# First attention of a four-layer gated cross-attention network: averaging normalised tokens with a folded Wv·Wo, and summing the weights in the exponential

## The reference

```python
xn = layer_norm(ctx, gamma_x, beta_x)                   # 64 context tokens of a sequence
ln = layer_norm(layernorm(x), gamma_l, beta_l)          # 64 latent tokens
q = (ln @ Wq).reshape(b, 64, 8, 64)                     # 8 heads of 64
k_x, v_x = split(xn @ Wkv); k_l, v_l = split(ln @ Wkv)
k_x = rope_rotate(k_x)                                  # k*cos + rotate_half(k)*sin, context keys only
k = concat([k_x, k_l]); v = concat([v_x, v_l])          # 128 keys and values of a sequence
out = softmax(q @ k.T / 8) @ v                          # per head
x = x + tanh(g_xattn[0]) * (out.reshape(b, 64, 512) @ Wo)
```

## Time and profile before

| what | value |
|---|---|
| median of 3 runs | 2398.12 us |
| profiled execution, its own time | 2399.08 us |
| its span | 2397.3 us |
| mean granted TensorE clock | 0.94 |
| busy over the span | PE 87%, DVE 79%, ACT 51%, POOL 14% |
| the first attention | 36 to 695 us, 64 tiles |
| in 52 to 690 us of it | PE busy 635.7 of 638 us, DVE 570.4, ACT 321.5, clock 1.00 |

### The profile page before, as it was taken

How to read it: one execution, slowest core, us unless ns; L and a number is a source line. 1 busy time by engine, 2 the same in 40 slices (tenths; PEclk the granted TensorE clock), 3 DMA queues, 4 the chain that set the end, 5 groups by cost and what they waited for, 6 DMA issues and landing times. The chain is left out here.

```text
span 2397.3 us, 51278 instructions
## 1 busy us (share of the span) xinstructions
PE 2076.7 (87%) x16365; PEld 1539.6 (64%) x16365; DVE 1888.4 (79%) x5125; ACT 1226.7 (51%) x2434; POOL 340.5 (14%) x680
## 2 busy tenths in 40 slices
PE   3999999999977888999998979699999987499507
PEld 3888888888853435777775757477777765244207
DVE  3899999999969898888885779566666668787785
ACT  1455555555533335677675646354544445307737
POOL 0111111111114443111111114100000022200000
PEclk9999999999988789999998989799999999699859
DMA  6111111111100000111110001112112111002442
GB/s 178 46 46 46 45 45 45 45 45 45 46 18 1 0 0 19 24 24 24 23 23 5 0 17 55 71 72 106 71 74 103 71 37 36 1 0 100 182 139 70
DMA packets 118317, 119.72 MB, mean 50 GB/s; under 512 B 45001, under 2 KB 101218, under 8 KB 116194
## 3 DMA queue, kind: packets, MB, share of 16 engines
q1 hardware_dynamic: 112248, 116.10, 16.0%
q10 hardware_dynamic: 5994, 2.70, 0.4%
HBM read 76.56 MB, written 25.43 MB: 43 GB/s over the span
## 5 line engine op out<-in xcount | busy, mean ns | idle before, releaser
L1658 DVE TENSOR_TENSOR arena<-arena 128x512 f32<-128x512 f32 (+1 forms) x256 | 171.1, 686 | 65.3 <-ACT arena L1696 59.7
L1696 ACT ACTIVATE arena<-banks,b1c 128x512 f32<-128x512 f32 x192 | 131.7, 687 | 168.4 <-PE banks L1571 168.2
L656 ACT ACTIVATE arena<-arena 128x512 f32<-128x512 f32 x128 | 80.8, 631 | 193.0 <-DVE arena L604 193.0
L888 PE MATMUL banks<-we,arena 128*128 128x512 f32 x256 | 141.5, 708 | 22.6 <-ACT arena L804 20.9
L1581 PEld LDWEIGHTS banks<-w2a,arena 128*128 128x128 f32 x1024 | 124.1, 192 | 28.7 <-issue 28.7
L217 DVE TENSOR_SCALAR xhat<-x_tiles,mean_var,rstd 128x128 f32 (+1 forms) x320 | 107.9, 374 | 33.6 <-POOL rstd L762 28.3
L1146 ACT ACTIVATE arena<-arena 128x512 f32<-128x512 f32 x128 | 80.7, 631 | 100.0 <-DVE arena L1098 100.0
L502 PE MATMUL banks<-arena 128*128 128x128 f32 x1024 | 131.3, 281 | 0.1
L1024 PE MATMUL banks<-arena 128*128 128x512 f32 x256 | 125.9, 615 | 3.9 <-ACT arena L1152 0.2
L1092 DVE TENSOR_REDUCE arena<-banks 128x8 f32<-128x512 f32 x128 | 87.7, 685 | 51.5 <-PE banks L1024 51.4
L518 PE MATMUL banks<-arena,wk 128*128 128x128 f32 x1024 | 126.6, 277 | 1.1 <-DVE arena L626 1.1
(11 more groups left out here) (271 smaller groups left out, 5402.1 us busy)
## 6 DMA issues: line engine op xcount, KB each, us to landing
arena<-coef_scratch SPq DMA_DIRECT2D x16, 2048.0 KB, 7.1
arena<-arena SPq DMA_DIRECT2D x128, 128.0 KB, 2.3
gated_scratch<-arena SPq DMA_DIRECT2D x16, 768.0 KB, 3.3
arena<-gated_scratch SPq DMA_DIRECT2D x16, 768.0 KB, 4.3
arena<-z1T_scratch SPq DMA_DIRECT2D x128, 64.0 KB, 2.2
arena<-ctxT_scratch SPq DMA_DIRECT2D x32, 256.0 KB, 2.8
arena<-in_ctx SPq DMA_DIRECT2D x64, 64.0 KB, 1.8
z1T_scratch<-arena SPq DMA_DIRECT2D x64, 64.0 KB, 1.5
```

The source lines that it names most:

```text
L888: mm = pe.matmul(ps[:, 6 + t.par if h else 2 + j, :], xTg[g.par][:, j * P:(j + 1) * P], k.we0[:, 4 * h:4 * h + 4, :].rearrange("p e m -> p ...
L1658: dve.tensor_tensor(hT[g.par][rows, c, :], hT[g.par][rows, c, :], wide_coef[g.par][rows, e, :], ALU.mult).then_inc(s["scaled"].sem, 1)
L1696: act.activation(hT[g.par][:, c, :], ps[:, HID + c % NHID, :], ACT.Gelu, bias=k.b1c[:, c:c + 1])\
```

## The change

It touches the first attention, its weights and their preparation.

- **Values and projection.** The values are no longer computed. For each head the kernel averages the 128 normalised tokens z (64 context, 64 latent) with the softmax weights, Y_h = z^T P_h^T, and multiplies by a folded matrix Wvo_h = Wv_h Wo_h (128x128). `prepare` makes the eight Wvo_h with 8 products and two copies.
- **Sums.** The exponential is now one ACTIVATE for each pair of heads, 128 columns each, four for each sequence: it reads the scores from PSUM, takes the negative scaled maximum as a bias column and writes the row sum by `accum_out`. VectorE no longer subtracts the maximum; it scales it (128x4), takes the reciprocal of the sums (128x4) and multiplies the weights by it before the transpose.
- **Queries.** QBD is zeroed once; ScalarE copies the two 64-row halves of the queries into it, VectorE's masked multiply goes.
- **Rotation.** The columns of Wq and Wk stay in their order, so the swap exchanges 32-row blocks: four transfers of 32 rows instead of two of 64; the signs of the sine table follow.
- **Context.** The transposed context comes in as an input (`ctxT`); its transpose, copy and store in the stage go.
- **Order.** The transposes of the weights, their use and the projection move one step later, x is updated another step later (lag 2 on VectorE), and the order within each body is new. VectorE's order in step s is: x of tile s-2, affine outputs of s+1, statistics of s+2, maxima and their scaling for both sequences of s, normalised x and context of s+2, `normalise(s, 0)`, cosine part of s+1, `normalise(s, 1)`, sine part and sum of s+1. ScalarE's order is that of the last hunk below.

```diff
@@ prepare
+        act.wait_ge(folded, 3)
+        for n in range(2):
+            act.activation(k.wvo0[:, n::2, :], ps[:, n, :].rearrange("p (h d) -> p h d", d=D), ACT.Copy)\
+                .then_inc(turned_sb, 1)
...
-        for dst, src in ((k.wq0, wq_raw), (k.wk0, wk_raw)):
-            to = dst[:, :].rearrange("p (c s h i) -> p s c h i", s=2, h=2, i=HD0 // 2)
-            of = src.rearrange("p (c h s i) -> p s c h i", s=2, h=2, i=HD0 // 2)
-            for half in range(2):
-                dve.tensor_copy(to[:, half], of[:, half]).then_inc(built, 1)
...
+        for h in range(H0):
+            rows = slice(h % 2 * HD0, h % 2 * HD0 + HD0)
+            mm = pe.matmul(ps[:, h % 2, h // 2 * D:(h // 2 + 1) * D], wvT[rows, h // 2, :], wo_raw[rows, h // 2, :],
+                           start=True, stop=True)
+        mm.then_inc(folded, 1)
@@ attention0, sync
-                sp.wait_ge(*s["ctxT_sb"](t))
-                sp.dma_start(k.ctxT_dram[t.idx], cto[t.par]).then_inc(k.ctxT_stored.at(t), 16)
                 sp.wait_ge(*s["kc"](t))
                 if t.has(1):
                     sp.wait_ge(*s["ksin"](t.back(1)))
-                for to, of in ((slice(0, 64), slice(64, P)), (slice(64, P), slice(0, 64))):
-                    sp.dma_start(kr[to, :], kc[of, :]).then_inc(swapped.at(t), 16)
+                for n in range(4):
+                    to, of = n * 32, (n ^ 1) * 32
+                    sp.dma_start(kr[to:to + 32, :], kc[of:of + 32, :]).then_inc(swapped.at(t), 16)
@@ attention0, gpsimd
+        pool.memset(QBD, 0.0).then_inc(preset, 1)
@@ attention0, tensor
+            if t := at(-1):
+                for b in range(PAIR):
+                    pe.wait_ge(*s["normed"](t, b + 1))
+                    if t.has(1):
+                        pe.wait_ge(*s["y_sb"](t.back(1), b + 1))
+                    for c in range(HPAIRS):
+                        mm = pe.transpose(ps[:, PT + b, c * P:(c + 1) * P], prob[:, b, c], k.ident)
+                    mm.then_inc(s["pt_psum"].sem, 1)
             if t := at(0):
                 pe.wait_ge(*s["krot"](t))
                 pe.wait_ge(*s["klat"](t))
                 pe.wait_ge(*s["qbd"](t))
+                if t.has(1):
+                    pe.wait_ge(*s["prob"](t.back(1)))
                 for b in range(PAIR):
                     for c in range(HPAIRS):
-                        mm = pe.matmul(ps[:, 6 + b, c * P:(c + 1) * P], QBD[:, c, b].rearrange("p h i -> p (h i)"),
+                        mm = pe.matmul(ps[:, S + b, c * P:(c + 1) * P], QBD[:, c, b].rearrange("p h i -> p (h i)"),
                                        KT[:, c, :, b, :], start=True, stop=True)
                     mm.then_inc(s["s_psum"].sem, 1)
...
+            if t := at(0):
+                if at(1):
+                    pe.wait_ge(*s["z_ready"](at(1)))
+                for b in range(PAIR):
+                    mm = pe.transpose(ps[:, TURN, (2 + b) * P:(3 + b) * P], Z[t.par][:, b].rearrange("p s i -> p (s i)"),
+                                      k.ident)
+                mm.then_inc(s["zn_psum"].sem, 1)
             if t := at(1):
                 pe.wait_ge(*s["z_ready"](t))
-                if t.has(2):
-                    pe.wait_ge(*s["pt_sb"](t.back(2)))
+                if t.has(3):
+                    pe.wait_ge(*f["x_updated"](t.back(3)))
+                if t.has(1):
+                    pe.wait_ge(*s["klat"](t.back(1)))
                 for n in range(2):
                     for c in range(HPAIRS):
-                        mm = pe.matmul(ps[:, n, c * P:(c + 1) * P], k.wk0[:, c * P:(c + 1) * P], Z[t.par][:, :, n],
+                        mm = pe.matmul(ps[:, KC + n, c * P:(c + 1) * P], k.wk0[:, c * P:(c + 1) * P], Z[t.par][:, :, n],
                                        start=True, stop=True)
                     mm.then_inc(s["k_psum"].sem, 1)
+            if t := at(-1):
+                pe.wait_ge(*s["zn_sb"](t))
+                for b in range(PAIR):
+                    pe.wait_ge(*s["pt_sb"](t, b + 1))
+                    pe.matmul(ps[:, PT + b, :], zn[t.par][:, b], probT[:, b], start=True, stop=True)\
+                        .then_inc(s["y_psum"].sem, 1)
+            if t := at(1):
+                if t.has(1):
+                    pe.wait_ge(*s["qbd"](t.back(1)))
                 for c in range(HPAIRS):
-                    mm = pe.matmul(ps[:, 3, c * P:(c + 1) * P], k.wq0[:, c * P:(c + 1) * P], Z[t.par][:, :, 1],
+                    mm = pe.matmul(ps[:, Q, c * P:(c + 1) * P], k.wq0[:, c * P:(c + 1) * P], Z[t.par][:, :, 1],
                                    start=True, stop=True)
                 mm.then_inc(s["q_psum"].sem, 1)
...
             if t := at(2):
                 pe.wait_ge(*f["xhat_ready"](t))
                 pe.wait_ge(*s["zhat"](t))
...
+                pe.transpose(ps[:, TURN, 0:P], k.xh[:, t.par, :], k.ident)
+                pe.transpose(ps[:, TURN, P:2 * P], zh[t.par], k.ident).then_inc(f["xT_psum"].sem, 1)
...
             if t := at(-1):
+                pe.wait_ge(*s["y_sb"](t))
                 if at(1):
                     pe.wait_ge(*s["kc"](at(1)))
...
                 for h in range(H0):
+                    mm = pe.matmul(ps[:, KC, 0:D], Y[:, h].rearrange("p b i -> p (b i)"), k.wvo0[:, h, :],
+                                   start=h == 0, stop=h == H0 - 1)
+                mm.then_inc(s["out_psum"].sem, 1)
         steps(pe, T, 2, 1, body)
@@ attention0, vector
+        def normalise(t, b):
+            dve.wait_ge(*s["prob"](t, (b + 1) * HPAIRS))
+            k.hold(dve)
+            dve.reciprocal(rec[:, b], ssum[:, b]).then_inc(s["srec"].sem, 1)
+            dve.wait_ge(*s["srec"](t, b + 1))
+            dve.tensor_tensor(prob[:, b], prob[:, b], rec[:, b].unsqueeze(2).broadcast_to([P, HPAIRS, P]), ALU.mult)\
+                .then_inc(s["normed"].sem, 1)
+        def body(at):
+            if t := at(-2):
+                dve.wait_ge(*s["out_psum"](t))
+                dve.scalar_tensor_tensor(out=k.x[:, t.idx, :], in0=ps[:, KC, 0:D], scalar=k.gates[:, 0:1],
+                                         in1=k.x[:, t.idx, :], op0=ALU.mult, op1=ALU.add)\
+                    .then_inc(f["x_updated"].sem, 1)
+            if t := at(1):
+                sl = t.par
+                if t.has(2):
+                    dve.wait_ge(*k.z1T_stored(t.back(2)))
+                    dve.wait_ge(*s["zn_psum"](t.back(2)))
+                    dve.wait_ge(*s["q_psum"](t.back(2)))
+                dve.wait_ge(*f["xT_psum"](t))
+                for dst, n, g in ((Z[sl][:, :, 0], 1, 0), (Z[sl][:, :, 1], 0, 2),
+                                  (z1o[sl].rearrange("p (b i) -> p b i", b=PAIR), 1, 4)):
+                    dve.tensor_scalar(dst, ps[:, TURN, n * P:(n + 1) * P].rearrange("p (b i) -> p b i", b=PAIR),
+                                      k.aff[:, g:g + 1], k.aff[:, g + 1:g + 2],
+                                      ALU.mult, ALU.add).then_inc(s["z_ready"].sem, 1)
             if t := at(2):
                 sl = t.par
                 dve.wait_ge(*ctx_loaded(t))
...
-                    dve.tensor_reduce(m, sc, AX.X, ALU.max).then_inc(s["smax"].sem, 1)
+                    dve.tensor_reduce(mx[:, b], ps[:, S + b, :].rearrange("p (c n) -> p c n", c=HPAIRS), AX.X, ALU.max)\
+                        .then_inc(s["smax"].sem, 1)
...
-                        .then_inc(s["sshift"].sem, 1)
+                    if t.has(1):
+                        dve.wait_ge(*s["prob"](t.back(1)))
+                    dve.tensor_scalar(nb[:, b], mx[:, b], -HD0 ** -0.5, None, ALU.mult).then_inc(s["nb"].sem, 1)
...
+            if t := at(0):
+                normalise(t, 0)
...
+            if t := at(0):
+                normalise(t, 1)
...
             if t := at(1):
                 dve.wait_ge(*swapped(t))
                 dve.tensor_tensor(rotB.rearrange("p (c i) -> p c i", i=SEQ), kr.rearrange("p (c i) -> p c i", i=SEQ),
                                   sinT, ALU.mult).then_inc(s["ksin"].sem, 1)
                 dve.wait_ge(*s["ksin"](t))
+                dve.wait_ge(*s["kcos"](t))
+                if t.has(1):
+                    dve.wait_ge(*s["s_psum"](t.back(1)))
                 dve.tensor_tensor(KT[:, :, 0], rotA.rearrange("p (c b i) -> p c b i", c=HPAIRS, b=PAIR),
                                   rotB.rearrange("p (c b i) -> p c b i", c=HPAIRS, b=PAIR), ALU.add)\
                     .then_inc(s["krot"].sem, 1)
-        steps(dve, T, 2, 1, body)
+        steps(dve, T, 2, 2, body)
@@ attention0, scalar (lines added and kept)
         k.ready(act)
+        act.wait_ge(preset, 1)
         def body(at):
             def weights(b):
                 if t := at(0):
+                    act.wait_ge(*s["nb"](t, b + 1))
+                    if t.has(1):
+                        act.wait_ge(*s["pt_psum"](t.back(1), b + 1))
+                        act.wait_ge(*s["srec"](t.back(1), b + 1))
+                    for c in range(HPAIRS):
```

(33 more changed lines are left out.)

172 lines of the change are left out of this document (38 added, 134 removed).

## The result

The kernel after takes 2433.16 us (median of 4 runs, 2432.34 to 2434.26) against 2398.36 us for the kernel before, timed in the same session: ratio 1.014, 95% interval 1.0127 to 1.0153. It is 34.8 us slower; forecast were 46, and the value lies inside the forecast case's own range (2412 to 2482). Its profiled execution took 2434.26 us with a span of 2432.5 us.

What follows compares the result with a forecast made beforehand. TensorE's queue bounds the kernel before; afterwards a ring through ScalarE's Y copies, the projection and VectorE was to set a 10.70 us step. 2399.1 + 4.6 + 63 x 0.66 = 2445.3, less 1.0: 2444 us, range 2382 to 2512.

Steps and rivals of the forecast that it cites:

- the forecast case: First attention's step between 10.2 and 11.3 us, total 2412 to 2482 us; chance 0.58.
- start of the first scores: Preparation ahead of the stage: extra products and copies, fewer weight copies; forecast + 2.1 us.
- The end of the stage: From the last scores to the end of x: 11.66 us before, 14.1 forecast after, + 2.5.
- Fixed together: Preparation and stage end outside the 63 steps: + 4.6 us, bounds 2 to 7.
- e: Distance between ScalarE's 128-column exponentials, including the accumulator read: taken as 0.39 us.
- The floor: Lowest e, with the accumulator read free: 0.257 us per exponential.
- the first ring: Maxima, eight exponentials, ScalarE copies through Y, projection, x, affine outputs, statistics: 7.58 + 8e, 10.70 us; forecast to set the step.
- The second ring: Maximum, four exponentials, z, kc, key swap, sine, sum, x, affine outputs, statistics: 6.98 + 4e + L, 10.44 us.
- L: Landing time of a key swap transfer of 64 KB: taken as 1.9 us, between 1.5 and 2.3.
- that rival's case: Accumulator read free and key swap decides: step 9.91 us, total 2394.5 us, no change; chance 0.15.
- TensorE at or near the bound: Rival: accumulator free and transfers landing in 1.5 us; step 9.64 us, total 2377.5, faster by 20; chance 0.14.
- A read that overlaps nothing: Rival: ScalarE's accumulator read fully exposed, e 0.48 to 0.59, step 11.42 to 12.30, total 2490 to 2545 us; chance 0.13.

Runs made afterwards that it cites:

- e9: Kernel after with a new TensorE order, early affine outputs, two Y buffers, later x update and kc before z, plus row sums left out: 2365.85 us.
- e1: Kernel after with the exponentials' accumulator left out (sums a constant 1, weights not normalised): 2408.47 us.
- e3: Kernel after without the accumulator and with two swap transfers of 64 rows (constant sums, wrong rows paired): 2377.09 us.
- e2: Kernel after with the keys swapped by two transfers of 64 rows instead of four of 32 (wrong rows paired): 2426.11 us.
- e7: Kernel before with the transposed context as an input, its transpose, copy and store removed: 2394.63 us, ratio 0.9978.
- e8: Kernel after, sums kept, with a new TensorE order, early affine outputs, two Y buffers, x update behind the key sum, kc before z: 2384.94 us.
- e10: e8 with keys of s+1 ahead of the scores of s, kc copied before all exponentials, projection in the latent keys' bank: 2430.35 us.
- e12: e10 with transposes of s+2 behind the averages, two buffers for transposed keys, latent keys copied before the exponentials: 2393.77 us.
- e5: Kernel after with early affine outputs, projection of tile s-2 behind the keys of s+1, x update behind the cosine part: 2551.05 us.

## Why the prediction was right, and where it was off

**The shape of the answer held.** TensorE's work fell from 10.02 to 9.53 us a step (9.54 forecast; e9 shows 9.45 where TensorE alone decides), and the time rose nevertheless, because rings through the in-order queues of ScalarE, SyncE and VectorE became longer than TensorE's work. TensorE's clock stayed at 0.99 to 1.00 in the stage and has no part in the difference, as forecast.

**The sum, term by term.** By the profiled executions: start of the first scores 53.76 - 52.3 = + 1.5 (+ 2.1 forecast). The end of the stage, from S(63) to the end of x, was 11.66 and is 730.96 + 0.35 - 716.74 = 14.57:

```profile
716.74 1.95 PE L513 MATMUL banks<-arena 128*128 128x128 f32 x16
...
728.87 2.05 PE L563 MATMUL banks<-wvo,arena 128*128 128x128 f32 x16 [0.69 <-ACT arena L691]
```
```profile
730.96 0.35 DVE L582 SCALAR_TENSOR_TENSOR x_tiles<-banks,gates,x_tiles 128x128 f32<-128x128 f32 x1 [5.56 <-PE banks L563]
```

That is + 2.9 (+ 2.5 forecast). Fixed together + 4.4 (4.6). The 63 steps add 63 x (10.523 - 10.025) = + 31.4 (63 x 0.66 = 41.6). 2399.1 + 4.4 + 31.4 is 2434.9, the execution took 2434.3.

**The step that was mis-sized is e.** I took 0.39 for an exponential with its accumulator read; it is 0.345. The floor was confirmed: without the accumulator an exponential takes 0.25 (e1), with it 0.09 more. The Trainium skill ("ScalarE: Activation LUTs", What ACT_TABLE_LOAD costs) led to 0.29 without a read; the runs have 0.25. With e = 0.345 the first ring of the prediction is 10.34 instead of 10.70, and it is no longer the longest.

**So the other ring decides.** The second ring was forecast as 6.98 + 4e + L. With 0.345 and L = 1.9 that is 10.26; the rows of one step give 10.45, and the difference is in one place: SyncE's four issues and the landing took 369.17 - 365.35 = 3.82 us, where 3 x 0.56 + 1.9 = 3.58 were forecast. The issues are 0.6 us apart instead of 0.56, L is 2.0. The prediction said that a wait for the swap in each step would put it in a rival; that sign came, since the two rings are so close that a tenth of a microsecond changes which one shows. It is not that rival's case, however: there the accumulator was free and the time 2394.5. e1 and e3 show that it is not free, and e2 shows that without the longer swap the forecast ring would decide 0.1 us lower.

**What was luck.** The path that the prediction named, through the Y copies and the projection, is not the one that decides. With e as measured, that path alone would have given 2399.1 + 4.6 + 63 x 0.30 - 1 = 2421.6 us, 23 slower where 35 were measured. Taking e 0.045 too high added 0.36 to that ring and stood in for the swap, which was taken 0.24 too short and left as the second. The direction, and that two rings would lie within some tenths of a microsecond of each other, were worked out; that the number came within 11 us of the measured one is partly two errors of opposite sign.

**The signs that were named.** TensorE idle about 1 us before the projection, released by ScalarE: came, 0.8 to 1.1. A small ScalarE instruction behind each exponential: came. Sine part within 0.3 us of the swap's landing: the fourth issue begins at about 365.35 + 1.8, lands 2.0 later at 369.15, and the sine part begins at 369.17. VectorE idle before x in each step: did not come in the kernel after, only in runs such as e2 and e3, where the swap is shorter. A step of 10.7: was 10.52.

**The rivals.** TensorE at or near the bound needed both a free accumulator and a shorter swap. e3 made such a case, by two transfers in place of a faster landing, and took 2377.09 us, where 2377.5 was worked out; in e3 the first ring and TensorE's own work are both within 0.2 us of the step. A read that overlaps nothing is excluded by e = 0.345.

**What stays open.** How much of the 6.9 us in e7 is gained, since its interval reaches from 3.1 to 7.4, and whether an order exists that takes the last 0.3 us of a step from e8 with the sums kept: e10 and e12 tried, and each met another ring.

## What to carry to other kernels

When work is taken off the engine that bounds a software pipeline, add up every ring that goes through its in-order queues, engine by engine, before counting the gain; here a 0.5 us saving a step turned into a loss of 0.5. Rings close to each other hide each other: single edits gave 25 and 7 us, both 56, so an edit that gives little may have uncovered its neighbour. A moved block makes rings of its own (e5, e10, e12 each met one), and the wait that VectorE or TensorE shows in each step names the place to go round from.

## What the runs showed of the hardware

- An accumulated row sum is not free: a separate instruction reads it, 0.19 to 0.26 us long by its rows, and it puts 0.09 us between starts of 128-column exponentials (0.25 to 0.345).
- Transfers from one part of the on-chip memory to another: four of 32 rows are issued 0.6 us apart and land 2.0 us after their issue, two of 64 rows are issued 0.56 apart and land after 2.3.
- TensorE's granted clock in e5: 0.81 and then 0.61 in the 5.5 us behind an idle time of 1.87 us, and 1.00 again in the 4.7 us after that. These are mixtures of the two levels of 1.2 and 2.4 GHz. The next idle time of 1.93 us was followed by no slower products (scores 2.05, keys 1.95), so the same idle time did not always bring the clock down. From 100 to 660 us it went on like this: in one step of three the scores took 2.05 us, in the other two 2.4 to 3.5 us. Idle times of 0.8 to 1.1 us a step left the clock at 1.00 in the kernel after.
